# Splitting one step's work over two: the centred input, a packed convolution and the results of the up products in a fused three-layer kernel

## The chip, the cores and the metric

The kernel runs on one core of one Trainium2 chip. The metric is the device time of one execution, in microseconds (us). The core has TensorE (PE; its weight loads are shown as PEld), VectorE (DVE), ScalarE (ACT), GpSimd (POOL) and the queue that issues most transfers (SP).

## The reference

The input has 4 sequences of 1024 positions with 128 features. Four residual layers follow one another: the block `attn_a`, a feed-forward layer of 8 experts, an attention layer, and the same feed-forward layer again. The change touches only `attn_a`:

```python
def _forward(x, ...):                       # x: the normalised input
    h = _ln(x, ln_conv_g, ln_conv_b)
    conv = grouped causal convolution of h  # 4 taps, 4 groups of 32 channels
    x = x + conv + conv_b
    h = _ln(x, ln_attn_g, ln_attn_b)
    q, k, v = h @ Wq.T + bq, h @ Wk.T + bk, h @ Wv.T + bv
    pooled_q = cumsum(q) / (1..S)
    pooled_k = cumsum(pooled_q * k) / (1..S)
    x = x + pooled_k * v
    h = gelu(_ln(x, ln_boom_g, ln_boom_b) @ Wb.T + bb)     # 128 -> 512
    return x + h @ Wu.T + bu                               # 512 -> 128
```

## The kernel before

**Tiles and chunks.** The 4096 tokens are 8 tiles of 512 (`NT`), two to a sequence. A feed-forward tile is worked through in 32 chunks (`CH`) of 128 hidden columns. Of each chunk, PE computes the gate and the up product (`gate_up`, lines 1119 to 1121, three matmuls each since every fp32 operand is split in a high and a low part), ACT makes silu of the gate (L1640), DVE multiplies it with the up product (`hid`, L2097), ACT rounds the product to its high part (`h_hi`, L1658), DVE subtracts to get the low part (`h_lo`, L2118), and PE accumulates the down product (`down`, lines 1126 to 1128).

**Pairs and steps.** The first feed-forward layer runs in four pairs of tiles, 64 steps to a pair. At step p each engine goes through its own list: PE does the extra work of the step, then `gate_up` of chunk p + 2, then waits for `h_lo` of chunk p and does `down` of chunk p. ACT does silu of chunk p + 1, `h_hi` of chunk p, then the extra work. DVE does the product of chunk p + 1, `h_lo` of chunk p, then the extra work. The instruction order on each engine is this hand-written one; semaphores tie the engines together.

**The extra work** of pair i (0, 1 and 2) is the block `attn_a` of sequence i + 1, written in `sequence_step`, whose stages are placed by tables: `AT` gives for each stage and for each half u of the sequence its step, `at(p, kind)` tells whether the stage is due at step p. In pair 0 (kind "first") 10 steps are added to each entry (`SHIFT_FIRST`). In pairs 1 and 2 (kind "middle") 3 steps are added (`TAPS_LATER`) to all stages but "tok", "T1" and "copy". Sequence 0 is computed before the pairs; there the stages are called one by one.

The stages that matter here:

- "tok": ACT writes the centred and doubly normalised input of a half, `hc_tok` (L1543, four instructions of 128x128), and DVE the once normalised input, `a0_tok` (L1927, four instructions). The first time, DVE also copies the statistics (`lns`, L1914), for which ACT waits.
- "T1": PE transposes both (L848); "copy": ACT copies one to `hT` (L1548), DVE the other to `a0T` (L1931).
- "conv": in pair 0 four matmuls a half from `hT` (L888). In pairs 1 and 2 it is packed: SP writes each half of `hT` to memory (L583) and reads it back as four shifted copies (`taps`, L586), and PE multiplies them in four narrow products (L878). "a1" adds the result on DVE (L1936), "T5" transposes it back, "stats5" takes its statistics.
- "up": PE's four products to the 512 hidden columns (L942), into two PSUM banks in turn. "hid1": DVE reads out the four of the second half (L1989). An up product c of that half waits for the read-out of product c - 2. "gelu" and "down" follow.

```python
AT = {"tok": (0, 1), "T1": (2, 4), "copy": (2, 4), "conv": (5, 6), "a1": (6, 7), "T5": (7, 8), ...
UP_AT = [AT["up"][0] + c for c in range(4)] + [AT["up"][1]] * 4     # AT["up"] = (32, 37)
    return UP_AT[4] - 1 if name == "hid1" else AT[name][u]
```

So in pairs 1 and 2 "tok" is at steps 0 and 1, the packed convolutions at 8 and 9, "a1" at 9 and 10, the second half's up products at 40 and their read-out at 39, the last thing that DVE does in that step. In pair 0 the same stages stand at 10 and 11, 15 and 16, 16 and 17, 47 and 46.

In pair 0, at step 12, DVE also takes the statistics of the next feed-forward tile (L1867) and POOL computes its root, and at step 13 POOL waits for all eight "tok" instructions of DVE, both halves (`a_tokd`), and then computes the low parts of the last quarter of the expert weights (`low_part`, L689, three instructions of 128x1024).

Of the kernel before, what the change touches and what calls it, by code (L numbers as in the profile page):

```python
# [140 lines left out]
def rests_by_pool(p):  # L141
# [9 lines left out]

AT = {"tok": (0, 1), "T1": (2, 4), "copy": (2, 4), "conv": (5, 6), "a1": (6, 7), "T5": (7, 8),
# [7 lines left out]

UP_AT = [AT["up"][0] + c for c in range(4)] + [AT["up"][1]] * 4
DOWN_AT = [AT["down"][0]] * 4 + [AT["down"][1] + c // 2 for c in range(4)]

SHIFT_FIRST = 10
NORM_AT = {"first": (12, 24), "middle": (10, 16), "last": (13, None)}
LOW_LATE = 13
LEFT = {"stats9": 0, "norm9": 2, "T10": 3, "h3": 3, "up": (4, 4, 5, 5), "hid1": (4, 4, 5, 5), "gelu": 6,
        "down": (8, 8, 9, 9), "y": 9, "T13": 10, "x1": 10}  # L170


def position(name, u, c=0):

    if name in ("up", "down"):
        return (UP_AT if name == "up" else DOWN_AT)[u * 4 + c]
    return UP_AT[4] - 1 if name == "hid1" else AT[name][u]


AHEAD_OF_TAPS, TAPS_LATER = ("tok", "T1", "copy"), 3  # L180


def at(p, kind):

    def now(name, u, c=0):
        later = 0
        if kind == "first":
            later = SHIFT_FIRST
        elif name not in AHEAD_OF_TAPS:
            later = TAPS_LATER  # L190
        return position(name, u, c) + later == p
    return now

# [4 lines left out]
def roots_to(b, name, u):  # L198

    if isinstance(b, int) and b == 0:  # L200
        return ROOTS_FIRST[name, u]
    return b * 16 - 6 + 4 * u + (4 if name == "norm5" else 12)


def left(p):
    def now(name, u, c=0):
        if u == 0 or name not in LEFT:
            return False
        return p == (LEFT[name][c] if name in ("up", "hid1", "down") else LEFT[name])
    return now  # L210


def only(*wanted):
    return lambda *stage: stage == wanted
# [14 lines left out]
def build(nc, ap):  # L229
    x_in, out = ap["hidden"], ap["out"]  # L230
    with ExitStack() as ctx:
        def sb(name, shape, dt=F32, stack=ctx):
            return stack.enter_context(nc.sbuf_tensor(name, shape, dt))
# [14 lines left out]
        later = sb("later", [P, 3, P + HALF], BF16)  # L248
# [123 lines left out]
        def bank(n):  # L372
            return ps[:, n, :]

        def xs(blk, n=1):

            return x[:, bass.ds(blk * P + NT, n * P)]

        def col(r):
            return par[:, r:r + 1]  # L380
# [217 lines left out]
        def _(pool):  # L598
# [155 lines left out]
            def ffn_beside_sequences(f):  # L754
# [5 lines left out]
                def pair(i, kind):  # L760
                    for p in range(2 * CH):
                        if kind == "first" and p == LOW_LATE:
                            pool.wait_ge(s["a_tokd"], 2 * BLK)
# [731 lines left out]
        def _(act):  # L1495
# [12 lines left out]
            def conv_matrices():  # L1508

                act.wait_ge(s["wraw_T"], 1)  # L1510
                a.copy(wt[:, T_CONV * P:12 * P], bank(4)[:, 3 * P:4 * P]).then_inc(s["wt_ready"], 1)
                a.copy(wt[:, 12 * P:T_IN * P], bank(7)[:, 0:3 * P]).then_inc(s["wt_ready"], 1)
# [15 lines left out]
            def sequence_step(b, now, first=False):  # L1528

                for u in range(2):  # L1530
                    ahead = first and u == 0
                    src, sl = bank(0 if ahead else 5 + u), slice(u * NT, (u + 1) * NT)
                    blocks = range(SUB * u, SUB * (u + 1))
                    if now("tok", u):

                        if first:
                            act.wait_ge(s["a_lnx"], 9 * (u + 1))
                        else:
                            act.wait_ge(s["a_lns"], b)
                            act.wait_ge(s["a_dn"], b * 2)  # L1540
                        ln = lnx if first else lns
                        for j in blocks:
                            a.activation(hc_tok[:, j * P:(j + 1) * P], xs(b * BLK + j), ACT.Identity,  # L1543
                                         bias=ln[:, L_BOTH_BIAS, j:j + 1],
                                         scale=ln[:, L_BOTH, j:j + 1]).then_inc(s["a_toka"], 1)
                    if now("copy", u):
                        act.wait_ge(s["a_T"], b * 2 + u + 1)
                        a.activation(hT[:, TAPS - 1 + u * NT:TAPS - 1 + (u + 1) * NT], bank(1 if ahead else 6),  # L1548
                                     ACT.Identity, bias=col(R_CONV_B), scale=col(R_CONV_G)).then_inc(s["a_hT"], 1)
                    for name, got, done in (("norm5", "a_pool", "a_n5"), ("norm9", "a_pool", "a_n9")):  # L1550
                        if now(name, u):
                            act.wait_ge(s[got], roots_to(b, name, u))
                            for j in blocks:
                                a.activation(a0_tok[:, j * P:(j + 1) * P], src[:, (j % SUB) * P:(j % SUB + 1) * P],
                                             ACT.Identity, bias=lna[:, 3, j:j + 1],
                                             scale=lna[:, 1, j:j + 1]).then_inc(s[done], 1)
                    for name, got, done, bias, scale in (("h2", "a_T7", "a_h2", R_ATTN_B, R_ATTN_G),
                                                         ("h3", "a_T10", "a_h3", R_BOOM_B, R_BOOM_G)):
                        if now(name, u):
                            act.wait_ge(s[got], b * 2 + u + 1)  # L1560
                            a.activation(h2T[:, sl], src, ACT.Identity, bias=col(bias),
                                         scale=col(scale)).then_inc(s[done], 1)
                    for c in range(4):
                        if u == 0 and now("up", 0, c):
                            act.wait_ge(s["a_up"], b * 8 + c + 1)
                            if first:
                                a.activation(gel_first[:, c, :], bank(c), ACT.Gelu,
                                             bias=col(R_BB + c)).then_inc(s["a_hid0"], 1)
                            else:
                                a.activation(gel[:, c, :], bank(5 + c % 2), ACT.Identity,  # L1570
                                             bias=col(R_BB + c)).then_inc(s["a_hid0"], 1)
                    if now("gelu", u):
                        act.wait_ge(s[f"a_hid{u}"], b * 4 + 4)
                        a.activation(gel[:, 4 * u:4 * u + 4, :], gel[:, 4 * u:4 * u + 4, :],
                                     ACT.Gelu).then_inc(s["a_gel"], 1)

            def first_step(*stage):
                sequence_step(0, only(*stage), True)
# [4 lines left out]
                for m in range(3):  # L1583
                    a.copy(w_hi[m][:, quarter], w_raw[m][:, quarter]).then_inc(s[f"split_hi{r}"], 1)

            first_step("tok", 0)
            conv_matrices()
            act.wait_ge(s["par_ready"], 1)
            first_step("copy", 0)
            high_part(0)  # L1590
            first_step("tok", 1)
            other_matrices()
            first_step("copy", 1)
            first_step("h2", 0)
# [242 lines left out]
        def _(dve):  # L1837
# [21 lines left out]
            def quarter_of_positions(n):  # L1859
                sl = slice(n * S // 4, (n + 1) * S // 4)  # L1860
                v.reciprocal(rinv[:, sl], cq[:, sl]).then_inc(s["rinv_ready"], 1)
# [47 lines left out]

            def sequence_step(b, now, first=False):  # L1910

                if now("tok", 0) and not first:

                    v.tensor_copy(lns[:], lnx[:, :, bass.ds(b * BLK, BLK)]).then_inc(s["a_lns"], 1)  # L1914
                    dve.wait_ge(s["a_lns"], b)
                for u in range(2):
# [1 line left out]
                    src, other = (bank(0), bank(1)) if ahead else (bank(5 + u), bank(6 - u))  # L1918
                    sl = slice(u * NT, (u + 1) * NT)
                    blocks = range(SUB * u, SUB * (u + 1))  # L1920
                    if now("tok", u):
                        if first:
                            dve.wait_ge(s["a_lnx"], 9 * u + 2)
                        for j in blocks:
                            mean = mvx[:, j, 0:1] if first else lns[:, L_MEAN, j:j + 1]
                            rstd = (lnx if first else lns)[:, L_RSTD, j:j + 1]
                            v.tensor_scalar(a0_tok[:, j * P:(j + 1) * P], xs(b * BLK + j), mean, rstd,  # L1927
                                            ALU.subtract, ALU.mult).then_inc(s["a_tokd"], 1)
# [71 lines left out]
            def first_step(*stage):  # L2000
                sequence_step(0, only(*stage), True)
# [3 lines left out]
                stats_of_input(u * SUB, u * SUB + SUB)  # L2005
            positions()
            quarter_of_positions(0)
            first_step("tok", 0)
            quarter_of_positions(1)
            parameters()  # L2010
            first_step("copy", 0)
            first_step("tok", 1)
            quarter_of_positions(2)
            dve.wait_ge(s["par_ready"], 1)
            first_step("a1", 0)
# [412 lines left out]
```

## Time and profile before

| | |
|---|---|
| time, median of 3 runs | 1781.38 us (1778.24 to 1783.17) |
| the profiled execution's own time | 1778.82 us |
| its span in the trace | 1777.1 us |
| pair 0, 1, 2 of the first feed-forward layer | about 65 to 252, 252 to 422, 422 to 591 us |
| the pair beside the projections of the attention | 591 to 760 us |
| attention, the second feed-forward layer beside it and after it | 760 to 1777 us |

In the trace each matmul of 512 columns is shown with its own duration, but they overlap: the next one starts 0.23 us after the last. An engine's idle time is put in brackets behind the instruction that ended it, with what released it.

### The profile page before, as it was taken

What the parts mean: (1) busy time and instruction counts of PE and PEld (TensorE: products, weight loads), DVE (VectorE), ACT (ScalarE), POOL (GpSimd) and SP (SyncE); (2) the same over time, 40 slices, a digit from 0 to 9 for tenths busy, and PEclk for the clock granted to TensorE, in tenths of its full rate; (3) what the DMA queues carried; (4) which work ended last, traced back from release to release, by engine and by line L of the source; (5) the groups of instructions that cost most, each with busy time, mean ns of one, the idle gap of its engine ahead of it and who ended that gap; (6) DMA issues with size and microseconds to landing.
All of it is one profiled execution on the core that took longest, in us unless ns stands there. A gap on an engine that the chain in (4) does not pass through costs nothing.

```text
span 1777.1 us, 27907 instructions
## 1 busy us (share of the span) xinstructions
PE 1691.1 (95%) x10265; PEld 1097.9 (62%) x10265; DVE 1257.4 (71%) x2134; ACT 1039.8 (59%) x1690; POOL 478.6 (27%) x647
## 2 busy tenths in 40 slices
PE   5799999999999999988889999999999999999998
PEld 3567676767677877633335555555555555558877
DVE  6677577766766777777877777777777777636665
ACT  6445755555565555567666666566666566665554
POOL 6522001200210123421114444434444443440000
PEclk8999999999999999989999999999999999999999
DMA  7000001002000123223010100000000000010000
GB/s 213 0 1 1 1 24 37 1 1 56 7 1 1 36 83 94 84 78 102 26 48 3 36 25 24 3 24 25 14 25 24 20 7 2 2 31 1 6 7 6
DMA packets 63427, 52.42 MB, mean 30 GB/s; under 512 B 7984, under 2 KB 58559, under 8 KB 63295
## 3 DMA queue, kind: packets, MB, share of 16 engines
q1 hardware_dynamic: 63120, 50.57, 10.0%
q8 instruction: 85, 1.39, 0.3%
q14 instruction: 48, 0.39, 0.1%
q10 hardware_dynamic: 174, 0.07, 0.0%
HBM read 32.40 MB, written 18.22 MB: 28 GB/s over the span
## 4 chain that ended last, share of the span: by engine, by line
PE 82%; DVE 7%; ACT 5%; issue 2%; DMA 1%; POOL 1%; SPq 0%; DVEq 0%; ACTq 0%; POOLq 0%
PE ps L1264 8%; PE ps L1227 7%; PE ps L1265 6%; PE ps L1266 6%; PE ps L1119 5%; PE ps L1120 5%; PE ps L1121 5%; PE ps L1092 4%; PE ps L1296 4%; PE ps L1061 3%; PE ps L1298 3%; PE ps L1297 3%; PE ps L848 3%; PE ps L1126 3%; PE ps L1128 3%; PE ps L1127 3%
## 5 line engine op out<-in xcount | busy, mean ns | idle before, releaser
L1634 ACT ACTIVATE pr<-ps 128x1024 f32<-128x1024 f32 (+2 forms) x285 | 268.0, 945 | 185.6 <-PE ps L1049 113.8
L2097 DVE TENSOR_TENSOR hid<-sg,ps 128x512 f32<-128x512 f32 x256 | 175.0, 683 | 192.0 <-PE ps L1121 144.6
L808 POOL TENSOR_TENSOR h_lo<-hid,h_hi 128x512 fp32r<-128x512 f32 x176 | 226.0, 1284 | 263.1 <-ACT h_hi L1734 258.6
L1640 ACT ACTIVATE sg<-ps 128x512 f32<-128x512 f32 x256 | 153.9, 601 | 240.6 <-PE ps L1121 238.2
L2087 DVE TENSOR_REDUCE negp<-ps 128x2 f32<-128x1024 f32 (+2 forms) x224 | 254.7, 1146 | 49.8 <-PE ps L1049 29.2
L1119 PE MATMUL ps<-xn_hi,w_hi 128*128 128x512 f32 x512 | 227.7, 445 | 2.2 <-DVE xn_lo L1890 2.2
L1264 PE MATMUL ps<-xn_hi,w_hi 128*128 128x512 f32 x512 | 223.1, 436 | 0.7 <-DVE hid L2224 0.6
L2224 DVE SCALAR_TENSOR_TENSOR hid<-sg,ps 128x512 f32<-128x512 f32 x176 | 121.1, 688 | 126.0 <-ACT sg L1724 125.3
L1121 PE MATMUL ps<-xn_hi,w_lo 128*128 128x512 f32 x512 | 202.0, 394 | 0.0
L1265 PE MATMUL ps<-xn_lo,w_hi 128*128 128x512 f32 x512 | 201.8, 394 | 0.0
L1120 PE MATMUL ps<-xn_lo,w_hi 128*128 128x512 f32 x512 | 201.8, 394 | 0.0
L1266 PE MATMUL ps<-xn_hi,w_lo 128*128 128x512 f32 x512 | 201.3, 393 | 0.0
L2118 DVE TENSOR_TENSOR h_lo<-hid,h_hi 128x512 fp32r<-128x512 f32 x236 | 176.3, 747 | 0.0
L1734 ACT CAST h_hi<-hid 128x512 fp32r<-128x512 f32 x256 | 157.5, 615 | 14.6 <-PE ps L1298 10.2
L1658 ACT CAST h_hi<-hid 128x512 fp32r<-128x512 f32 x256 | 157.6, 616 | 0.6 <-DVE hid L2097 0.4
L1724 ACT ACTIVATE sg<-ps 128x512 f32<-128x512 f32 x176 | 105.5, 599 | 76.8 <-PE ps L1266 75.5
L1227 PE MATMUL ps<-pr,vp 128*9 128x512 f32 (+3 forms) x1376 | 144.7, 493 | 0.0
L1092 PEld LDWEIGHTS ps<-qs,ks 63*128 63x128 bf16 x720 | 35.1, 93 | 166.7 <-issue 140.6
L1092 PE MATMUL ps<-qs,ks 63*128 63x512 bf16 (+2 forms) x720 | 113.9, 334 | 13.8 <-DVE negp L2087 9.8
L2230 DVE TENSOR_TENSOR hid<-hid,ps 128x512 f32<-128x512 f32 x176 | 120.3, 684 | 6.3 <-PE ps L1266 3.1
L1264 PEld LDWEIGHTS ps<-xn_hi,w_hi 128*128 128x128 f32 x512 | 95.9, 187 | 40.4 <-issue 18.7
L1119 PEld LDWEIGHTS ps<-xn_hi,w_hi 128*128 128x128 f32 x512 | 97.0, 189 | 36.6 <-issue 17.3
(244 smaller groups left out, 3090.9 us busy)
## 6 DMA issues: line engine op xcount, KB each, us to landing
qs<-qd SPq DMA_DIRECT2D x60, 96.0 KB
ks<-kd SPq DMA_DIRECT2D x60, 96.0 KB
kd<-qkp SPq DMA_DIRECT2D x14, 256.0 KB, 2.9
qd<-qkp SPq DMA_DIRECT2D x7, 384.0 KB, 2.6
w_raw<-in_Wg SPq DMA_DIRECT2D x4, 512.0 KB, 7.2
w_raw<-in_Wu SPq DMA_DIRECT2D x4, 512.0 KB, 7.5
w_raw<-in_Wd SPq DMA_DIRECT2D x4, 512.0 KB, 8.9
work<-hd SPq DMA_DIRECT2D x8, 256.0 KB, 4.7
```

Of the source, the lines that this page charges most:

```text
L808: g.tensor_tensor(h_lo[:, q % 2, :], hid[:, q % 4, :], h_hi[:, q % 2, :].bitcast(F32), ALU.subtract).then_inc(FS[1]["hlo_pool"], 1)
L1092: mm = pe.matmul(dst[e], k_of(n)[r, hp, j * P:(j + 1) * P], q_of(n)[r, hp, from_q:from_q + w], start=True, stop=st not in MASKED)
L1119: pe.matmul(dst, w_hi[m][:, w], xn_hi[:, h, :], start=True, stop=False)
L1120: pe.matmul(dst, w_hi[m][:, w], xn_lo[:, h, :], start=False, stop=False)
L1121: pe.matmul(dst, w_lo[m][:, w], xn_hi[:, h, :], start=False, stop=True).then_inc(f[sig], 1)
L1227: mm = pe.matmul(ps[32 * h:32 * h + HD + 1, O_BANK, from_q:NT], vp[:, n % 2, j, h, :], pr_of(n, st)[:, h, 0:NT - from_q], start=(j == 0), ...
L1264: pe.matmul(dst, w_hi[m][:, w], xn_hi[:, h, :], start=True, stop=False)
L1265: pe.matmul(dst, w_hi[m][:, w], xn_lo[:, h, :], start=False, stop=False)
L1266: pe.matmul(dst, w_lo[m][:, w], xn_hi[:, h, :], start=False, stop=True).then_inc(f[sig], 1)
L1634: a.activation(pr_of(n, st)[:].rearrange("p (e a) q -> p e a q", e=2)[:, :, hps[0]:hps[-1] + 1, 0:WIDTH[st]], heads(buf, hps, WIDTH[st]), ...
L2087: v.tensor_reduce(to[:, :, hps[0]:hps[-1] + 1, i % SUB], heads(buf, hps, JOB_WIDTH[k]), AX.X, ALU.max, negate=True).then_inc(T["reduced"], 1)
L2118: v.tensor_tensor(h_lo[:, c % 2, :], hid[:, c % 4, :], h_hi[:, c % 2, :].bitcast(F32), ALU.subtract).then_inc(f["hlo"], 1)
```

## The change

Three things are moved; no arithmetic is changed.

1. "tok" has a second index c: each half is done in two pieces of two 128x128 instructions on ACT and on DVE. In pairs 1 and 2 the pieces stand at steps 0 and 1 (first half) and 2 and 3 (second half), in pair 0 at 10 to 13. Before, each half was one piece of four at steps 0 and 1 (10 and 11). ACT's and DVE's waits stand ahead of each piece.
2. In pairs 1 and 2 the packed convolution of the second half is at step 10 instead of 9. Its "a1" stays at 10, its "T5" at 11.
3. "hid1" of up products 2 and 3 stands one step later than that of 0 and 1: at step 40 in pairs 1 and 2, at 47 in pair 0. The up products are not moved.

```diff
-AT = {"tok": (0, 1), "T1": (2, 4), "copy": (2, 4), "conv": (5, 6), "a1": (6, 7), "T5": (7, 8),
+AT = {"T1": (2, 4), "copy": (2, 4), "conv": (5, 6), "a1": (6, 7), "T5": (7, 8),
+TOK_AT = ((0, 1), (2, 3))
...
-    return UP_AT[4] - 1 if name == "hid1" else AT[name][u]
+    if name == "tok":
+        return TOK_AT[u][c]
+    if name == "hid1":
+        return UP_AT[4 + c] - 1 + c // 2
+    return AT[name][u]
...
         elif name not in AHEAD_OF_TAPS:
-            later = TAPS_LATER
+            later = TAPS_LATER + (name == "conv" and u == 1)
...
@@ ACT, sequence_step
-                    if now("tok", u):
-
+                    for c in range(2):
+                        if not now("tok", u, c):
+                            continue
                         if first:
                             act.wait_ge(s["a_lnx"], 9 * (u + 1))
                         else:
                             act.wait_ge(s["a_lns"], b)
                             act.wait_ge(s["a_dn"], b * 2)
                         ln = lnx if first else lns
-                        for j in blocks:
+                        for j in blocks[2 * c:2 * c + 2]:
...
@@ DVE, sequence_step
-                if now("tok", 0) and not first:
+                if now("tok", 0, 0) and not first:
...
-                    if now("tok", u):
+                    for c in range(2):
+                        if not now("tok", u, c):
+                            continue
                         if first:
                             dve.wait_ge(s["a_lnx"], 9 * u + 2)
-                        for j in blocks:
+                        for j in blocks[2 * c:2 * c + 2]:
...
```

For sequence 0, ahead of the pairs, ACT and DVE call the two pieces of each half one right behind the other.

## Rows read from the trace of the kernel before

**Rows 1.** The page, part 1: busy us, share of the span, instructions of each engine
```profile
PE 1691.1 (95%) x10265; PEld 1097.9 (62%) x10265; DVE 1257.4 (71%) x2134; ACT 1039.8 (59%) x1690; POOL 478.6 (27%) x647
```

**Rows 2.** Waits of PE, 95 to 640 us: waiter, releaser, us in total, times, longest us
```profile
PE ps L1126 <- DVE h_lo L2118: 4.4, 7, 1.1
...
PE ps L1126 <- ACT h_hi L1658: 2.2, 3, 0.7
...
PE ps L878 <- DMA taps<-hd: 2.2, 2, 1.1
```

**Rows 3.** Timeline, pair 1: start us, us, engine, line, operation, tiles, records, idle before
```profile
253.37 1.65 ACT L1543 ACTIVATE work<-x,lns 128x128 f32<-128x128 f32 x4
...
254.93 0.58 ACT L1640 ACTIVATE sg<-ps 128x512 f32<-128x512 f32 x1
...
256.21 0.68 DVE L2118 TENSOR_TENSOR h_lo<-hid,h_hi 128x512 fp32r<-128x512 f32 x1
...
257.04 0.47 PE L1126 MATMUL ps<-h_hi,w_hi 128*128 128x512 f32 x1 [1.00 <-DVE h_lo L2118]
...
258.89 0.78 ACT L1548 ACTIVATE hT<-ps,par 128x512 f32<-128x512 f32 x1 [0.34 <-PE ps L848]
...
259.59 0.60 ACT L1640 ACTIVATE sg<-ps 128x512 f32<-128x512 f32 x1
...
260.90 0.68 DVE L2118 TENSOR_TENSOR h_lo<-hid,h_hi 128x512 fp32r<-128x512 f32 x1
...
262.17 0.40 PE L1126 MATMUL ps<-h_hi,w_hi 128*128 128x512 f32 x1
```

**Rows 4.** Timeline, pair 0, 105 to 115 us
```profile
105.97 1.11 DVE L1927 TENSOR_SCALAR work<-x,lns 128x128 f32<-128x128 f32 x4
...
106.20 0.48 PE L1126 MATMUL ps<-h_hi,w_hi 128*128 128x512 f32 x1 [1.12 <-DVE h_lo L2118]
...
108.06 0.78 ACT L1548 ACTIVATE hT<-ps,par 128x512 f32<-128x512 f32 x1 [0.34 <-PE ps L848]
...
109.12 0.86 DVE L1867 BATCH_NORM_STATS2 st<-x 128x6 f32<-128x128 f32 x4
...
110.88 0.68 DVE L2118 TENSOR_TENSOR h_lo<-hid,h_hi 128x512 fp32r<-128x512 f32 x1
...
111.81 5.17 POOL L689 TENSOR_TENSOR w_lo<-w_raw,w_hi 128x1024 fp32r<-128x1024 f32 x2
...
112.14 2.60 DVE L2118 TENSOR_TENSOR h_lo<-hid,h_hi 128x512 fp32r<-128x512 f32 x1
...
114.89 0.48 PE L1126 MATMUL ps<-h_hi,w_hi 128*128 128x512 f32 x1
```

**Rows 5.** Timeline, pair 1, 277 to 281 us
```profile
277.00 1.06 PE L878 MATMUL ps<-taps,w_taps 128*32 128x512 f32 x8 [1.04 <-DMA taps<-hd]
...
277.99 0.50 PE L1119 MATMUL ps<-xn_hi,w_hi 128*128 128x512 f32 x1
...
280.19 0.60 PE L848 MATMUL ps<-ident,a0T 128*128 128x128 f32 x4
...
280.90 0.74 DVE L1936 SCALAR_TENSOR_TENSOR a0T<-ps,par,a0T 128x512 f32<-128x512 f32 x1
```

**Rows 6.** Timeline, pair 1, 361 to 365 us
```profile
361.34 0.60 ACT L1640 ACTIVATE sg<-ps 128x512 f32<-128x512 f32 x1
...
362.01 1.61 DVE L1989 TENSOR_SCALAR work<-ps,par 128x512 f32<-128x512 f32 x2 [0.36 <-PE ps L942]
...
363.54 0.68 DVE L2097 TENSOR_TENSOR hid<-sg,ps 128x512 f32<-128x512 f32 x1
...
364.13 0.68 DVE L2118 TENSOR_TENSOR h_lo<-hid,h_hi 128x512 fp32r<-128x512 f32 x1
...
364.96 0.47 PE L1126 MATMUL ps<-h_hi,w_hi 128*128 128x512 f32 x1 [0.74 <-ACT h_hi L1658]
```

**Rows 7.** Windows: window, us; busy us (instructions) of PE, PEld, DVE, ACT, POOL; PEclk, DMA share, GB/s
```profile
760.00:920.00 160.00, 133.48 (x1532) 55.22 (x1530) 123.26 (x159) 106.89 (x141) 31.32 (x87) 0.96 0.22 64
```

More of the change, by code:

```diff
@@ L1584, in high_part @@
                     a.copy(w_hi[m][:, quarter], w_raw[m][:, quarter]).then_inc(s[f"split_hi{r}"], 1)
-            first_step("tok", 0)
+            for c in range(2):
+                first_step("tok", 0, c)
             conv_matrices()
@@ L1590, in _ @@
             high_part(0)
-            first_step("tok", 1)
+            for c in range(2):
+                first_step("tok", 1, c)
             other_matrices()
@@ L1920, in sequence_step @@
                     blocks = range(SUB * u, SUB * (u + 1))
-                    if now("tok", u):
+                    for c in range(2):
+                        if not now("tok", u, c):
+                            continue
                         if first:
                             dve.wait_ge(s["a_lnx"], 9 * u + 2)
-                        for j in blocks:
+                        for j in blocks[2 * c:2 * c + 2]:
                             mean = mvx[:, j, 0:1] if first else lns[:, L_MEAN, j:j + 1]
@@ L2007, in _ @@
             quarter_of_positions(0)
-            first_step("tok", 0)
+            for c in range(2):
+                first_step("tok", 0, c)
             quarter_of_positions(1)
@@ L2011, in _ @@
             first_step("copy", 0)
-            first_step("tok", 1)
+            for c in range(2):
+                first_step("tok", 1, c)
             quarter_of_positions(2)
```

## The prediction

> **What bounds the kernel now.** I began with the page: PE is busy 95% of the span [rows 1], so a piece of work that is moved on ACT or DVE is worth something only where PE stands still for it. Therefore the second view was PE's own waits in the stretch that holds the three pairs with a sequence beside them [rows 2]. Down products (L1126) wait 4.4 us for `h_lo` and 2.2 us for `h_hi`, and the packed convolution waits 2.2 us for its transfer, in two waits. The third view was the timeline around each wait, to see which entry of the step tables causes it. Three kinds touch the change. At "tok", PE stands still for 1.00 us in pair 1 [rows 3] and 1.12 us in pair 0 [rows 4]. At the second packed convolution it waits 1.04 us for the taps [rows 5]; the two waits of this line sum to 2.2 us [rows 2]. Behind the up products of the second half it waits 0.74 us [rows 6], three times, which is the `h_hi` line of [rows 2]. Pairs 1 and 2 run the same lists, so I work one of them out and count it twice. The rest of the 4.4 us is three waits and one more of 0.2 us or so that the change leaves alone.
>
> **The convolution one step later.** PE is at this convolution at 277.00 - 1.04 = 275.96 us and the taps come at 277.00 [rows 5]. Moved, it stands behind the rest of step 9, which takes 280.19 - 277.99 = 2.20 us, and behind the "T5" of the first half (at most its 0.60 us). PE then gets to it at about 278.6 without a wait, 1.5 us after the transfer. SP's queue is not changed: it issues the same transfers on the same `hT`, which comes earlier exactly as much as PE does. So the whole wait goes: 1.04 us and, for both pairs, 2.2 us [rows 2]. What is late next: "a1" of this half stays in step 10. DVE started it 280.90 - 280.19 = 0.71 us after that step's first PE work; now it waits for a convolution that itself starts 0.4 to 0.6 us into the step and takes 1.06, so it starts at about 1.65, 0.95 us later, and behind it on DVE are the statistics of the next tile, the product of chunk 12 and `h_lo` of chunk 11. But PE's own step has grown by the same convolution, 277.99 - 277.00 = 0.99 us, so PE comes to "down" of chunk 11 0.99 us later too, and no new wait arises. Bounds: nothing repaid, or at worst 0.5 us repaid in each pair (DVE's 0.95 with half of PE's 0.99 as cover). I take nothing repaid, since both figures come from adjacent rows. Gain 2.2 us, at least 1.2.
>
> **The last read-outs behind the next product.** In pair 1 DVE reads out up products 2 and 3 from 362.01 and only then multiplies chunk 41, at 363.54, though silu of that chunk began at 361.34 [rows 6]. A product follows its silu by some 0.68 us (0.60 and the release), so it can start at 362.02. `h_lo` comes 0.59 later, at 362.61, and "down" follows the start of `h_lo` by 364.96 - 364.13 = 0.83 us: it is ready at 363.44. PE itself is ready at 364.96 - 0.74 = 364.22. The wait goes whole, 0.74 us. The two read-outs, 1.53 us by 363.54 - 362.01, now run from 363.20 to 364.73, so the product of chunk 42 starts at 364.73 and its `h_lo` at 365.32, ready for PE at 366.15. PE gets there one plain step after the down product of chunk 40: 364.22 and nine matmuls of 0.23 us, 366.3. It is covered, narrowly (0.15 us). PE's up products 2 and 3 wait for read-outs 0 and 1, which don't move; "gelu" and "down" come four and five steps later. In pair 0 the tables give the same order with the same wait. Gain 3 x 0.74 = 2.2 us; bounds 1.5 (0.25 repaid in each by the narrow cover) and 2.2.
>
> **"tok" in pieces, pairs 1 and 2.** ACT takes four 128x128 pieces between 253.37 and 254.93, 0.39 us each, ahead of the next silu; `h_lo` then starts at 256.21 and PE waits 1.00 us [rows 3]. With two pieces everything is 0.78 us earlier: `h_lo` at 255.43, "down" ready at 256.26 against PE's own 256.04. Gain 0.78, 0.22 us of wait left. But the other pieces don't vanish. In step 2 ACT now has two of them behind the copy: the copy would start at 258.89 - 0.78 = 258.11, silu of chunk 4 follows 0.70 later plus 0.78 for the pieces, at 259.59, exactly where it was. `h_lo` of chunk 3 comes 256.21 - 254.93 = 1.28 after its silu, at 260.87, "down" is ready at 261.70. PE, 0.78 us earlier than the 262.17 of before, would be there at 261.39: a new wait of 0.31 us. In step 1 and step 3 ACT has no copy beside the two pieces, and I find no wait. Net 0.47 us in a pair; ACT and DVE also get repeated waits, whose signals are long there, so I take 0.45, twice: 0.9 us. Bounds: 0 (ACT gives back all that it saved, since its work in steps 0 to 3 is the same) and 0.78.
>
> **"tok" in pieces, pair 0.** The first gain is the same 0.78 us, but here POOL takes part. Before, DVE's statistics started at 109.12 [rows 4], so the copy ahead of them at about 108.5. With PE 0.78 us earlier the transposes release it at 108.06 - 0.78 = 107.28; copy 0.60 and two pieces of 1.11 / 4 = 0.28 put the statistics at 108.44, 0.68 us earlier. `h_lo` of chunk 13 then starts at 110.20 instead of 110.88, and the last two pieces stand behind it: they end at 110.20 + 0.60 + 0.56 = 111.36. POOL waits for exactly these before its weight work, so it starts at about 111.4, against 111.81. While POOL ran, the next `h_lo` (from 112.14) took 2.60 us instead of 0.68: it ended at 114.74, 0.35 after POOL's first instruction (111.81 + 5.17 / 2 = 114.40), and "down" followed at 114.89. So the gain behind this place is POOL's 0.4 us and not 0.78. The Trainium skill's page "SBUF — State Buffer", section "Who interferes with whom", says that a DVE instruction with two SBUF inputs and a GpSimd instruction that reads SBUF exclude one another for a whole instruction. The trace agrees, 2.60 us against 0.68; by that rule the sum takes 0.4 here, and without it it would take the 0.68 of DVE's chain. Bounds 0 (POOL starts where it did) and 0.78.
>
> **Sequence 0.** The pieces run back to back; only repeated waits are added, on signals already there. I cost it at nothing, at most 0.1 us.
>
> **The sum.** 2.2 + 2.2 + 0.9 + 0.4 = 5.7 us off the profiled execution's 1778.8 (span 1777.1, 1.7 us around it), or 0.32%. PE works nearly without a gap from there to the end, so the saving reaches it. That execution lies 2.6 us under the median of the runs, 1781.38, and within their spread of 4.9; off the median I forecast 1775.7 us. Within 0.3%, or 5.3 us, is about what a measurement here can't tell from no change, so the sum stands at the edge of it.
>
> **Rivals.**
> (a) The pieces of "tok" only move the wait. For it: ACT's total in steps 0 to 3 is unchanged, and 0.31 us of new wait is already worked out. Against: ACT's lists of steps 1 and 3 have room. Then 2.2 + 2.2 = 4.4 us, 1777.0. Chance 0.18.
> (b) The late convolution or the read-outs repay: DVE's lists in steps 10 and 41 are full, and the covers are 0.04 and 0.15 us. With both lower bounds: 1.2 + 1.5 + 1.3 = 4.0 us, 1777.4. Chance 0.13.
> (c) "tok" gains in full, because ACT's order leaves less delay than I added up: 4.4 + 3 x 0.78 = 6.7 us, 1774.7. Chance 0.13.
> (d) Slower, by the granted clock at the start of the attention. There, 760 to 920 us, it was 0.96 on average [rows 7], 6.4 us lost of 160, with PE much less dense (133.48 us busy). If the earlier arrival changed where these drops lie and their loss grew, the gain would be eaten; it decides from a second such loss (5.7 - 6.4, 1782.1), and it takes 11 us, 1786.7, to be slower by more than 0.3%. Nothing in the change acts on that stretch, so 0.04.
> (e) That the change does nothing at one of its places, as when the taps come later by the step that they were given: the transfer depends on `hT` alone, which speaks against it. 2.2 us less, 1777.9. Chance 0.04.
>
> **How the numbers follow.** The forecast as summed has 0.48. Two thirds of it (0.33) lie above 5.3 us, and with (c) and a little of measurement spread on (a) and (b), faster by over 0.3% has 0.50; slower 0.04; the rest, 0.46, is within. The bounds of the terms give 2.7 us (1.2 + 1.5) to 6.8 us, thus 1774.6 to 1778.7 off the median; the median's own spread of some 2 us on either side widens that to 1772.7 to 1780.6.
>
> **What would show it.** In the changed trace: the wait of L878 for the taps gone in both pairs; the 0.74 us waits behind L1989 gone in all three; the wait at "tok" down to some 0.2 us, with a new one of about 0.3 two steps later; in pair 0 the weight work of POOL some 0.4 us earlier relative to the start of its pair. DVE's "a1" of the second half should show an idle time of about 1 us. The prediction is wrong if PE shows new waits in steps 11 to 13 or at step 41, or if the stretch from 760 us on differs by more than 1 us.

## The result, and the profile after

Six runs of each kernel: 1769.78 us median after (1769.63 to 1770.91), 1782.01 before (1778.19 to 1783.17). The ratio is 0.9938, 95% interval 0.9925 to 0.9951: 11.0 us faster by the ratio, 12.2 by the medians. The forecast of 1775.7 us was too high and its range, 1772.7 to 1780.6, did not hold the time. The changed kernel's profiled span is 1768.1 us, 9.0 under that of before.

PE's waits in the stretch of the pairs, as in [rows 2] (waiter, releaser, us in total, times, longest):

```profile
PE ps L1131 <- DVE h_lo L2130: 2.8, 9, 0.4
PE ps L853 <- ACT work L1560: 0.5, 3, 0.2
```

The waits for the taps and for `h_hi` are gone, those for `h_lo` fell from 4.4 to 2.8 us. The second line, 0.5 us in three waits, stands in the trace of before as well (there L848 <- ACT L1554). By these sums the change saved 6.0 us, close to the forecast 5.7. The span fell by 9.0 and the medians by 12.2, so either the waits don't tell the whole cost, or time went elsewhere. Both are true, as the following shows.

**"tok", pair 1**, against [rows 3] (start us, us, engine, line):

```profile
247.44 0.88 ACT L1549 ACTIVATE work<-x,lns 128x128 f32<-128x128 f32 x2
...
248.23 0.58 ACT L1648 ACTIVATE sg<-ps 128x512 f32<-128x512 f32 x1
...
249.51 0.68 DVE L2130 TENSOR_TENSOR h_lo<-hid,h_hi 128x512 fp32r<-128x512 f32 x1
249.73 0.39 PE L1126 MATMUL ps<-xn_hi,w_lo 128*128 128x512 f32 x1
...
250.34 0.47 PE L1131 MATMUL ps<-h_hi,w_hi 128*128 128x512 f32 x1 [0.23 <-DVE h_lo L2130]
...
252.87 0.86 ACT L1549 ACTIVATE work<-x,lns 128x128 f32<-128x128 f32 x2
...
253.64 0.58 ACT L1648 ACTIVATE sg<-ps 128x512 f32<-128x512 f32 x1
...
254.93 0.68 DVE L2130 TENSOR_TENSOR h_lo<-hid,h_hi 128x512 fp32r<-128x512 f32 x1
...
255.23 0.40 PE L1126 MATMUL ps<-xn_hi,w_lo 128*128 128x512 f32 x1
...
255.75 0.47 PE L1131 MATMUL ps<-h_hi,w_hi 128*128 128x512 f32 x1
```

Silu of chunk 2 comes 0.79 us after "tok" begins and no longer 1.56, and PE's wait is down from 1.00 to 0.23. Two steps on, silu stands behind the pieces, `h_lo` of chunk 3 starts at 254.93, and the down product starts at 255.75, 0.52 us after the matmul ahead of it (255.23) and not 0.23. That is the new hold of 0.3 us that was forecast, but no bracket shows it: a matmul is drawn 0.40 us long while the next can start 0.23 after it, so the first 0.17 us of each hold are covered by the drawing. The 0.12 us that are left got no bracket either; the shortest bracket in the rows of this text is 0.23 us.

**Pair 0**, against [rows 4]:

```profile
106.14 0.60 DVE L1937 TENSOR_SCALAR work<-x,lns 128x128 f32<-128x128 f32 x2
...
106.82 5.17 POOL L694 TENSOR_TENSOR w_lo<-w_raw,w_hi 128x1024 fp32r<-128x1024 f32 x2 [0.30 <-DVE work L1937]
...
107.25 2.50 DVE L2130 TENSOR_TENSOR h_lo<-hid,h_hi 128x512 fp32r<-128x512 f32 x1
...
109.90 0.47 PE L1131 MATMUL ps<-h_hi,w_hi 128*128 128x512 f32 x1 [0.32 <-DVE h_lo L2130]
```

POOL starts when the last pieces end, and `h_lo` behind it takes 2.50 us, as forecast.

**The convolution**, against [rows 5]:

```profile
271.54 0.60 PE L853 MATMUL ps<-ident,a0T 128*128 128x128 f32 x4
...
272.07 1.07 PE L883 MATMUL ps<-taps,w_taps 128*32 128x512 f32 x8
...
273.07 0.50 PE L1124 MATMUL ps<-xn_hi,w_hi 128*128 128x512 f32 x1
...
273.21 0.75 DVE L1946 SCALAR_TENSOR_TENSOR a0T<-ps,par,a0T 128x512 f32<-128x512 f32 x1 [0.87 <-PE ps L883]
```

No wait for the taps, and "a1" idles 0.87 us on DVE, starting 1.67 after the step's first PE work (1.65 was forecast).

**The read-outs**, against [rows 6]:

```profile
353.59 0.60 ACT L1648 ACTIVATE sg<-ps 128x512 f32<-128x512 f32 x1
...
354.29 0.69 DVE L2109 TENSOR_TENSOR hid<-sg,ps 128x512 f32<-128x512 f32 x1 [0.39 <-ACT sg L1648]
...
355.50 1.40 DVE L1999 TENSOR_SCALAR work<-ps,par 128x512 f32<-128x512 f32 x2
...
356.07 0.40 PE L1126 MATMUL ps<-xn_hi,w_lo 128*128 128x512 f32 x1
...
356.31 0.39 PE L1131 MATMUL ps<-h_hi,w_hi 128*128 128x512 f32 x1
```

The product follows its silu by 0.70 us, the read-outs stand behind `h_lo`, and PE runs on 0.24 us after the matmul ahead.

**Where the time went, step by step.** DVE starts one product (`hid`, L2097 before, L2109 after) for each chunk. The start in a changed kernel less the start of the same product in the first trace of before is its lead; how the lead grows between plain steps is what a place is worth. All kernels of this study stand in one table, in us; a minus is time saved. (For each trace the rows are the same; in before, the stretches end at products at 88.4, 100.5, 135.9, 198.6, 237.3, 249.9, 270.0, 344.2, 377.1, 419.2, 439.2, 513.5 and 546.5 us.)

| kernel | lead at 88 us | 88 to 100 | tok, pair 0 | read-outs, pair 0 | tok, pair 1 | conv., pair 1 | read-outs, pair 1 | tok, pair 2 | conv., pair 2 | read-outs, pair 2 | the named places |
|---|---|---|---|---|---|---|---|---|---|---|---|
| changed, first trace | -1.83 | -2.79 | -0.39 | -0.94 | -0.41 | -1.41 | -0.96 | -0.39 | -1.48 | -0.96 | -6.94 |
| changed (e4_all) | 1.43 | -2.81 | -0.37 | -0.94 | -0.42 | -1.39 | -0.97 | -0.41 | -1.46 | -0.97 | -6.93 |
| changed (e8_all_again) | -1.70 | -2.79 | -0.37 | -0.96 | -0.41 | -1.36 | -0.98 | -0.40 | -1.43 | -0.96 | -6.87 |
| e1_tok | -0.36 | -2.81 | -0.38 | | -0.42 | -0.08 | | -0.40 | -0.12 | | -1.40 |
| e2_conv | -0.20 | -2.81 | | | | -1.42 | | | -1.49 | | -2.91 |
| e3_readouts | 0.74 | 0.02 | | -0.98 | | -0.40 | -0.97 | | 0.00 | -0.96 | -3.31 |
| e7_before_again | 1.34 | -2.80 | | | | -0.28 | | | -0.30 | | -0.58 |
| e5_second_half_at_3 | -1.04 | -2.81 | -0.37 | -0.94 | -0.78 | -1.39 | -1.01 | -0.76 | -1.45 | -0.96 | -7.66 |
| e6_one_and_three | -0.76 | -2.79 | -0.68 | -1.00 | -1.17 | -1.37 | -1.01 | -1.15 | -1.46 | -0.95 | -8.79 |
| e9_one_and_three_again | -0.31 | -2.79 | -0.68 | -0.96 | -1.16 | -1.39 | -0.94 | -1.13 | -1.42 | -0.95 | -8.63 |

Empty cells are 0.04 or less. The places give the changed kernel 6.9 us, and the same 6.9 in each of its three traces. The cells under "conv." of the kernels that leave the convolution alone (e1_tok, e3_readouts, e7_before_again) are the scatter of its wait for the taps between executions, 0 to 0.40 us. The first trace of before has the longest such waits of the four traces that leave the convolution alone; the other three spent 0.58, 0.20 and 0.40 us less on them. Against the mean of the four, the change is worth 6.6 us and not 6.9.

**The other part of the 9.0 us.** The spans of the first two traces differ by 9.0 us: 1.8 ahead of 88 us, 2.8 from 88 to 100, 6.9 at the places, and 2.5 us given back behind the last product of the first feed-forward layer (at 760.53 in before, at 748.99 in the changed kernel). From that product to the end before takes 1016.6 us, the changed kernel 1019.1. The difference lies where TensorE's clock was at its lower level. Windows of before and of the changed kernel (us; busy us and instructions of PE, PEld, DVE, ACT, POOL; granted clock, DMA share, GB/s):

```profile
740.00:950.00 210.00, 179.99 (x1844) 83.24 (x1842) 160.42 (x215) 133.68 (x183) 49.64 (x108) 0.97 0.22 63
```

```profile
740.00:950.00 210.00, 181.85 (x1833) 82.28 (x1832) 157.13 (x204) 136.28 (x185) 46.50 (x105) 0.95 0.19 54
```

In these 210 us the granted clock was at its lower level, 0.50 or 1.2 GHz, for 13.7 us in both traces of before and for 20.5 us in all three of the changed kernel. Over all eleven traces the time from that product to the end goes with this figure, whatever was moved: 1016.6 to 1017.0 us where it is 13.7 (both of before, e3_readouts, e5_second_half_at_3), 1018.2 at 17.1 (e6_one_and_three), 1018.5 to 1019.1 at 20.5 (e2_conv and the changed kernel), 1020.7 at 23.9 (e1_tok, e9_one_and_three_again).

### The profile page after: what moved, and what is told of

It reads as the page before. It is cut to its first block, busy times and chain, and to the rows that moved or that the text cites. A ratio compares the mean times of both kernels' runs of the same rounds, so it can differ in the third digit from the quotient of the medians.

```text
span 1768.1 us, 27913 instructions
## 1 busy us (share of the span) xinstructions
PE 1689.2 (96%) x10265; PEld 1097.0 (62%) x10265; DVE 1256.4 (71%) x2134; ACT 1038.8 (59%) x1690; POOL 478.1 (27%) x647
## 3 DMA queue, kind: packets, MB, share of 16 engines
q8 instruction: 85, 1.39, 0.3%
## 4 chain that ended last, share of the span: by engine, by line
PE 83%; DVE 8%; ACT 5%; issue 2%; POOL 1%; SPq 0%; DMA 0%; DVEq 0%; ACTq 0%; POOLq 0%
PE ps L1269 8%; PE ps L1232 7%; PE ps L1270 6%; PE ps L1271 6%; PE ps L1124 6%; PE ps L1126 6%; PE ps L1125 6%; PE ps L1097 4%; PE ps L1301 4%; PE ps L1066 3%; PE ps L1303 3%; PE ps L1302 3%; PE ps L853 3%; PE ps L1131 3%; PE ps L1133 3%; PE ps L1132 3%
## 5 line engine op out<-in xcount | busy, mean ns | idle before, releaser
L2109 DVE TENSOR_TENSOR hid<-sg,ps 128x512 f32<-128x512 f32 x256 | 174.7, 683 | 181.2 <-PE ps L1126 131.9
L1269 PEld LDWEIGHTS ps<-xn_hi,w_hi 128*128 128x128 f32 x512 | 95.9, 187 | 40.4 <-issue 18.7
L1066 PE MATMUL ps<-ks,qs 60*128 60x512 bf16 (+2 forms) x720 | 113.5, 331 | 6.2 <-DVE xn_lo L2226 2.6
```

Of the source, the lines that this page charges most:

```text
L1269: pe.matmul(dst, w_hi[m][:, w], xn_hi[:, h, :], start=True, stop=False)
```

## The experiments

**First session: one part at a time.** All four were timed against before, 34 runs of which had a median of 1778.87 us (1774.34 to 1783.36).

*e1_tok*: before, with only the pieces of "tok".

```diff
+TOK_AT = ((0, 1), (2, 3))
...
-                    if now("tok", u):
+                    for c in range(2):
+                        if not now("tok", u, c):
+                            continue
...
-                        for j in blocks:
+                        for j in blocks[2 * c:2 * c + 2]:
```

> Only the centred input is in pieces; the convolution and the read-outs stand as before. Theory A (each place gives what the traces of before and after show from step to step, and the rest of the measured 12 us is time at TensorE's lower clock, which is not tied to a part): the trace gains about 0.3 us at each of the three places, 0.9 us in all, and the total moves by that plus or minus a few us with the low stretches ahead of 100 us and at 760 us. Theory B (the pieces, which alone touch the work ahead of the pairs, remove the low stretch that lay at 88 to 96 us, and are worth most of the surplus): 4 to 6 us faster than before.

Measured: 1776.55 us, ratio 0.9981 (0.9969 to 0.9993), 2.3 us by the medians, short of theory B's 4 to 6. The place is worth 0.38, 0.42 and 0.40 us, 1.2 us in all where theory A had 0.9. The low stretch at 88 to 96 us was absent, as theory B has it, but it was absent from the next kernel too.

*e2_conv*: before, with only the convolution moved.

```diff
-            later = TAPS_LATER
+            later = TAPS_LATER + (name == "conv" and u == 1)
```

> Only the second half's packed convolution is a step later. Theory A: 1.4 us in each of pairs 1 and 2, 2.8 us in the trace behind 422 us (the waits shown were 1.04 and 1.12, and a wait costs some 0.3 more than is shown as idle), with the same plus or minus by low stretches. Theory B: 2.2 to 2.8 us faster in every run and no change ahead of 252 us.

Measured: 1776.23 us, 0.9983 (0.9970 to 0.9997); 1.42 and 1.49 us in the table. This kernel gives every engine the instructions of before up to 252 us, and yet it is 2.8 us ahead at 100 us. So that lead is not the change's. Theory B of the first two runs falls.

*e3_readouts*: before, with only the read-outs moved.

```diff
-    return UP_AT[4] - 1 if name == "hid1" else AT[name][u]
+    if name == "hid1":
+        return UP_AT[4 + c] - 1 + c // 2
+    return AT[name][u]
```

> Only the read-outs of up products 2 and 3 stand a step later. Theory A: 1.0 us in each of the three pairs, 3.0 us in the trace (shown waits 0.74 each). Theory B, as I forecast: 0.74 each, 2.2 us. The total moves by that plus or minus the low stretches.

Measured: 1777.00 us, 0.9993 (0.9979 to 1.0006), which alone would be no difference; in the trace 0.98, 0.97 and 0.96 us. Theory A holds, and the 0.74 of theory B was too small.

*e4_all*: the changed kernel.

> The changed kernel once more, on the chip and beside the runs of the other three. Theory A: the three pairs give 6.9 us again in the trace, and the total differs from that by the low stretches ahead of 100 us and at 760 us, which may lie otherwise than in the first profile: 7 to 12 us faster than before. Theory B: 12 us again, the low stretch at 88 to 96 us absent again.

Measured: 1772.45 us, 0.9963 (0.9952 to 0.9974), 6.4 us by the medians, a little less than theory A's 7 to 12 and far from theory B's 12, with the places unchanged at 6.93. The intervals of the two measurements of the same pair of kernels (0.9925 to 0.9951, and this) do not even touch, though no step differs.

**Second session: before again, and "tok" otherwise.** Before: 17 runs, 1777.66 us median (1774.80 to 1782.77).

*e7_before_again*: before, unchanged, one run.

> The kernel before, once more, for its trace. Theory A (the low stretches lie by chance): its three pairs run step for step as in the first trace, and the time ahead of 100 us or between 750 and 930 us differs by 0.5 to 4 us. Theory B (the low stretches belong to a kernel's code): the same stretches as in the first trace, among them the one at 88 to 96 us, and a time within 0.5 us of 1778.8.

Measured: 1776.79 us. The windows (us; busy us and instructions of PE, PEld, DVE, ACT, POOL; granted clock, DMA share, GB/s) of 85 to 100 us, first of the first trace of before, then of this one and of e2_conv:

```profile
85.00:100.00 15.00, 12.06 (x34) 7.39 (x33) 4.53 (x7) 6.07 (x9) 0.00 (x0) 0.77 0.01 1
```

```profile
85.00:100.00 15.00, 12.05 (x48) 8.23 (x48) 5.85 (x10) 8.32 (x11) 0.00 (x0) 1.00 0.00 1
```

```profile
85.00:100.00 15.00, 12.06 (x48) 8.31 (x47) 6.98 (x13) 7.27 (x12) 0.00 (x0) 1.00 0.00 1
```

The granted clock was 0.77 over these 15 us in one execution of before and 1.00 in the other. In the first trace PE had idled 2.94 us up to 89.83 (it waits there for ACT's gelu of sequence 0), and its next matmuls came 0.43 us apart, the lower level of 1.2 GHz, until 95.5; then 0.23 us apart. In this execution the same idle time came and no low level followed it. The low stretch cost 2.80 us, by the table, and it lies there or not in executions of one and the same kernel. Of the rest, the start up to 88 us differs by 1.34 us. It arises at 15 to 18 us (1.7 us, of which 0.4 are gained back later), in the matmuls of sequence 0's convolution (L888), of which 14 to 18 us holds eight in the first trace and four in this one:

```profile
14.84 3.70 PE L888 MATMUL ps<-hT,wt 128*128 128x512 f32 x8 [0.93 <-ACT hT L1548]
```

```profile
14.91 3.65 PE L888 MATMUL ps<-hT,wt 128*128 128x512 f32 x4 [0.93 <-ACT hT L1548]
```

They start 0.43 us apart there and 0.85 here, up to 18.4 us. The clock column of the profile reads 1.00 for these 4 us in both, so that this is the lower level again is read from the starts alone. The same slow start is in e4_all, which is 1.43 us behind at 88 us. The low stretches behind 760 us, 10.2 and 3.4 us long, did come again in this execution, as theory B has it. The wait for the taps also differs between executions: 2.2 us in two waits in the first trace, here

```profile
PE ps L878 <- DMA taps<-hd: 1.6, 2, 0.8
```

*e5_second_half_at_3*: the changed kernel, with

```diff
-TOK_AT = ((0, 1), (2, 3))
+TOK_AT = ((0, 1), (3, 3))
```

> The changed kernel with both pieces of the second half's centred input at step 3 (13 in pair 0), so that step 2 holds none beside the copy. Theory A (in the changed kernel the pieces that stand behind ACT's copy in step 2 make silu of chunk 4 late, and PE is held before the down product of chunk 3, a hold of 0.3 us that the profile doesn't even show as a wait): that hold goes in pairs 1 and 2, 0.3 us more gain in each than the changed kernel in the trace. Theory B (ACT's total over steps 0 to 3 decides, so a piece moved from step 2 is paid in step 3): no difference, or a new wait at the down product of chunk 4. The total can't tell 0.6 us apart; the steps in the trace can.

Measured: 1771.37 us, 0.9971 (0.9960 to 0.9983); 0.78 and 0.76 us at the place in pairs 1 and 2 where the changed kernel has 0.41 and 0.39. PE's start that was 0.52 us behind the one ahead of it in step 3 is now 0.22 behind. So the hold that the profile doesn't show was real and was worth 0.37, and ACT had room in step 3 for four instructions. In pair 0 the place stays at 0.37.

*e6_one_and_three*: that kernel, with the first half cut otherwise.

```diff
+TOK_CUT = (0, 1, 4)
...
-                        for j in blocks[2 * c:2 * c + 2]:
+                        for j in blocks[TOK_CUT[c]:TOK_CUT[c + 1]]:
```

> As the one before, and the first half cut into one 128x128 instruction at step 0 and three at step 1. Theory A: silu of chunk 2 is another 0.39 us earlier, PE's remaining wait of 0.23 us at the down product of chunk 1 goes too, and the whole place is worth 1.1 to 1.25 us in each of pairs 1 and 2, against 0.43 in the changed kernel: 1.4 to 1.6 us more in the two. Theory B: the three instructions at step 1 make the product of chunk 3 late and PE waits at the down product of chunk 2; no more than 0.5 us in each pair. If A holds this is the fastest version, 8 to 9 us under before by the steps of the trace, plus or minus the low stretches.

Measured: 1771.52 us, 0.9963 (0.9949 to 0.9976); 1.17 and 1.15 us at the place, as theory A had it. The medians don't show it as faster than e5_second_half_at_3 (1771.37); only the places do, 8.8 against 7.7 us. Its timeline in pair 1, the down product of chunk 1 at 250.65:

```profile
248.13 0.49 ACT L1550 ACTIVATE work<-x,lns 128x128 f32<-128x128 f32 x1
...
248.53 0.58 ACT L1649 ACTIVATE sg<-ps 128x512 f32<-128x512 f32 x1
...
249.52 1.27 ACT L1550 ACTIVATE work<-x,lns 128x128 f32<-128x128 f32 x3
...
249.82 0.68 DVE L2131 TENSOR_TENSOR h_lo<-hid,h_hi 128x512 fp32r<-128x512 f32 x1
...
250.42 0.39 PE L1127 MATMUL ps<-xn_hi,w_lo 128*128 128x512 f32 x1
...
250.65 0.47 PE L1132 MATMUL ps<-h_hi,w_hi 128*128 128x512 f32 x1
...
254.20 1.65 ACT L1550 ACTIVATE work<-x,lns 128x128 f32<-128x128 f32 x4
...
255.54 0.39 PE L1127 MATMUL ps<-xn_hi,w_lo 128*128 128x512 f32 x1
...
255.78 0.40 PE L1132 MATMUL ps<-h_hi,w_hi 128*128 128x512 f32 x1
```

PE goes from the up product to the down product in 0.23 us in step 1 and 0.24 in step 3, so nothing is left to gain there. In pair 0, behind POOL's weight work, it is 0.68 and not 1.17. There the gain follows the start of that work: with each trace's lead ahead of the place taken off, POOL starts at 111.81 in both traces of before, 0.37 us earlier in the changed kernel (gain 0.38) and 0.67 earlier in this one (gain 0.68).

**Third session: the two again.** Before: 11 runs, 1779.75 us median (1777.32 to 1782.39).

*e8_all_again*: the changed kernel, unchanged.

> The changed kernel a third time, in a session of its own. Theory A (its three pairs save 6.9 us, and what a median shows beyond or below that is where low stretches of TensorE's clock fell): 5 to 9 us faster, and among runs with the same mean granted clock 6 to 8 us faster. Theory B (the change also removes time that no step of the pairs shows, as the first measurement of 12 us has it): 10 to 13 us faster again.

Measured: 1770.66 us, 0.9949 (0.9937 to 0.9961), 9.1 us by the medians, just above theory A's 5 to 9 and under theory B's 10 to 13; places 6.87.

*e9_one_and_three_again*: the kernel of e6_one_and_three, unchanged.

> The version with one and three pieces, both of the second half at step 3, again. Its three pairs save 8.8 us in the trace. Theory A: 7 to 10 us faster than before, 1 to 2.5 us faster than the changed kernel at the same mean granted clock. Theory B: as fast as the changed kernel.

Measured: 1770.71 us, 0.9950 (0.9934 to 0.9967), 9.0 us by the medians and level with the changed kernel's 1770.66; places 8.63. At the same mean granted clock it is 1.3 to 2.5 us faster than the changed kernel, by the table that follows.

**The runs by their clock.** Each run comes with PE's mean granted clock. The runs of one kernel that share it lie close together (us, number of runs; levels outside these five are left out):

| mean granted clock | before | changed | one and three |
|---|---|---|---|
| 0.986 | 1782.5 (7) | | 1772.5 (1) |
| 0.987 | 1781.3 (7) | 1774.4 (2) | 1771.9 (1) |
| 0.988 | 1779.5 (11) | 1772.4 (2) | 1770.9 (4) |
| 0.989 | 1777.6 (26) | 1771.0 (16) | 1769.7 (1) |
| 0.990 | 1776.5 (4) | 1769.8 (2) | 1768.2 (2) |

In each row the changed kernel is 6.6 to 7.1 us faster. With one straight line for all kernels, a step of 0.001 is worth 1.4 us, and at the same clock the changed kernel is 6.8 us faster than before (e1_tok 1.2, e2_conv 3.1, e3_readouts 2.8, e5_second_half_at_3 7.1), and the version with one and three 8.5. The places that each kernel changes give 6.9 (e1_tok 1.2, e2_conv 2.9, e3_readouts 2.9, e5_second_half_at_3 7.7) and 8.7. That agrees to 0.3 us but for e5_second_half_at_3, with 9 runs, which is 0.6 off. Single runs scatter about the line by 0.9 us, and the clock is given to 0.001. The rest of every median goes with where low stretches fell.

## Why the prediction was wrong

- **Its places, order and signs were right.** All three parts save time, nothing new stands in steps 11 to 13 or at step 41, and the one new hold came at the step and with the size that were forecast (0.31 forecast, 0.29 by PE's starts). One of its own signs of being wrong did come: the stretch behind 760 us was to differ by no more than 1 us, and it is 2.5 us longer in the first trace of the changed kernel (2.1 and 2.3 in the other two). That is the mechanism of rival (d), at a smaller size than its 6.4, which was a sum of lost clock and not of time: 6.8 us more at the lower level cost these 2.5 us.
- **"tok"** was forecast at 0.45, 0.45 and 0.4 us; it measured 0.42, 0.40 and 0.38. Rival (c), the full gain, did not happen; its 0.78 in a pair takes e5's placing, and the whole hold, 1.17, takes e6's. POOL's share in pair 0 went as reckoned: it started 0.37 us earlier relative to the pair than before (106.82 against 111.81, with 4.62 us of lead ahead of the place). The rule that was weighed there (the Trainium skill, "SBUF — State Buffer", "Who interferes with whom") again agrees with the row, 2.50 us for an `h_lo` beside POOL. The two instructions of POOL that I took for half of 5.17 us each took 2.38 and 2.82, which changes nothing in the sum.
- **The read-outs** were forecast at 0.74 each and measured 0.96. Mis-sized was the price of a wait. PE went 364.96 - 363.82 = 1.14 us from one matmul's start to the next where 0.23 is normal, and the matmul behind the wait takes another 0.08 (364.96 to 365.27 instead of 0.23): 0.99 us, of which the bracket shows 0.74. I took the bracket for the cost. In the trace of before:

```profile
363.82 0.40 PE L1121 MATMUL ps<-xn_hi,w_lo 128*128 128x512 f32 x1
364.96 0.47 PE L1126 MATMUL ps<-h_hi,w_hi 128*128 128x512 f32 x1 [0.74 <-ACT h_hi L1658]
365.27 0.41 PE L1127 MATMUL ps<-h_lo,w_hi 128*128 128x512 f32 x1
```

- **The convolution** was forecast at 1.04 to 1.12 and measured 1.41 and 1.48. In pair 1, PE's own starts show 1.10 us gained by 283 us. The other 0.25 came at the down product of chunk 77 in the layer's count, at 288.95 in before: it starts 0.46 us after the matmul ahead of it and in the changed kernel 0.22. DVE was late there, by too little for a bracket to appear:

```profile
288.12 0.69 DVE L2118 TENSOR_TENSOR h_lo<-hid,h_hi 128x512 fp32r<-128x512 f32 x1
...
288.49 0.40 PE L1121 MATMUL ps<-xn_hi,w_lo 128*128 128x512 f32 x1
288.95 0.47 PE L1126 MATMUL ps<-h_hi,w_hi 128*128 128x512 f32 x1
```

  This hold stands in pairs 1 and 2 of all four traces that leave the convolution alone, and in none of the seven that move it. I had reckoned that PE's step grows by 0.99 and DVE's list by 0.95, so that nothing is repaid, and had not asked what the growth gives back. Rival (b) had the wrong sign.
- **The sum** of the places is thus 6.9 us where 5.7 was forecast. Against the profiled execution, 1778.8, that is 1771.9. The medians of the three later sessions are 1778.6 (62 runs of before) and 1771.9 (16 of the changed kernel), 6.7 us apart.
- **The step that failed** is the last: "off the median I forecast 1775.7 us", with "the median's own spread of some 2 us on either side". With 6.9 in the sum the forecast would have been 1774.5 us, inside the range, so the mis-sized holds are not what put the time outside. I took the sum off a median of three runs that was 2.8 us above the median of the 62, and let a spread of 2 us stand for runs that reach over 9. Of the miss of 5.9 us, 2.8 are this base, 1.0 is the sum (5.7 against 6.7) and 2.1 are the six runs after, which lie that much under the 16 later ones. The low stretches were in my sight, but only as rival (d), at one place, on the slower side alone. Shown since: they come and go ahead of 100 us too, 2.80 us at 88 to 96, in executions of the same code, and pull both medians. Of the first measurement's 12.2 us, some 6.8 belong to the change. The other 5.4 I put down to six runs of before with more such time than six runs after: 1782.0 us is a time of runs at 0.986 to 0.987 in the table, and the six after were at 0.989 and 0.990. The clock of those six runs of before is not on record, so this part is argued and not shown.
- **What stays open**: whether the changed kernel meets low stretches less or more often. 16 of its 22 runs lie at 0.989 and none below 0.987, against 26 and 11 of 62 for before; but the version with one and three, with more time saved at the same places, has 4 of 13 below 0.987. Behind 740 us it is the other way round: 20.5 us at the lower level in three traces of the changed kernel, 13.7 in two of before, yet 13.7 in e5_second_half_at_3, which differs by one step. No experiment here moves a low stretch at will.

## What to carry to other kernels

Price a hold of a pipelined engine by the starts of its instructions on both sides, not by the idle time that the profile draws: here the waits at the read-outs cost 0.22 to 0.25 us more than their bracket, the one at "tok" 0.17 (1.17 for 1.00), the one for the taps 0.06 by PE's starts (1.10 for 1.04), and holds of 0.23 and 0.29 us had no bracket at all. When a change is worth less than the runs of one kernel scatter, take its size from the same step in several traces, and compare medians only among runs with the same granted clock. At one place here, chunk 77, a full instruction list on another engine was relieved when the step that it runs beside grew longer, so ask of a moved piece what its new place covers as well as what it delays.

## What the runs showed of the hardware

TensorE's clock is granted differently to the same code: after the same 3 us of idle time the next 6 us ran at 1.2 GHz in two traces (the first of before, and e3_readouts) and at 2.4 GHz in the nine others. In one and the same kernel (e6_one_and_three, e9_one_and_three_again) the granted clock was at its lower level between 740 and 950 us for 17.1 us in one execution and for 23.9 in the other, and the time from the last product of the first feed-forward layer to the end was 1018.2 and 1020.7 us. A run's whole time moves by 1.4 us for each 0.001 of mean granted clock, and the runs of before alone spread from 0.985 to 0.991.
